# Attention over three layers: scores from 32-row matmuls in four row groups, split probabilities turned by DMA

## The reference

```python
x = x + L0(x)   # softmax(q k^T / sqrt(32)) modulated per head by sigmoid(tanh(..) ..), plus a field term; out @ Wout.T
x = x + L1(x)   # scores = where(mask, -inf, q k^T * scale); softmax; @ v; @ Wo.T; RMS norm of the output, gain and shift
x = x + L2(x)   # norm of x first, softmax attention, @ Wo.T; then a gated MLP behind a second norm
x = x + L3(x)   # quaternion rotation and spectral gate

def _attention(x, Wq, Wk, Wv, Wo):
    q, k, v = (x @ Wq.T), (x @ Wk.T), (x @ Wv.T)      # reshaped to heads
    p = softmax(einsum('blhd,bmhd->bhlm', q, k) / scale)
    return einsum('bhlm,bmhd->blhd', p, v) @ Wo.T
```

## Time and profile before

| | us |
|---|---|
| median of 2 runs | 3087.95 |
| the profiled execution | 3084.3 |
| its span, first to last instruction | 3082.5 |
| PE busy in the span | 2981.2 (97%) |
| DVE busy | 2096.0 (68%) |
| ACT busy | 1394.7 (45%) |
| POOL busy | 621.2 (20%) |
| mean granted PE clock | 0.982 of full speed |

### The profile page before, as it was taken

One profiled execution on the slowest core, in us unless ns is written; L12 is line 12 of the kernel. 1 busy time (PEld: TensorE's weight loads), 2 busy tenths in 40 slices (PEclk: granted clock), 3 DMA queues, 4 the chain that ended last, 5 costly groups with the idle time before them and its releaser, 6 DMA issues. The chain is left out here.

```text
span 3082.5 us, 67681 instructions
## 1 busy us (share of the span) xinstructions
PE 2981.2 (97%) x25333; PEld 2690.0 (87%) x25333; DVE 2096.0 (68%) x3768; ACT 1394.7 (45%) x2236; POOL 621.2 (20%) x434
## 2 busy tenths in 40 slices
PE   6999999999999999989999999599999999999997
PEld 5999999999999999978999999488888888888886
DVE  5777677767788888888888887554454454665554
ACT  3444444445566666666666665332222242222221
POOL 1122212222211111132211112022222221111111
PEclk7999999999999999999999999699999999999999
DMA  5443444345454454544555554322111241111101
GB/s 169 115 110 101 111 107 107 101 116 149 119 134 126 126 135 125 140 131 132 133 138 132 137 131 122 111 99 69 55 55 54 69 138 53 42 41 55 54 28 41
DMA packets 198920, 317.05 MB, mean 103 GB/s; under 512 B 42112, under 2 KB 99584, under 8 KB 198304
## 3 DMA queue, kind: packets, MB, share of 16 engines
q1 hardware_dynamic: 196512, 307.25, 36.2%
q10 hardware_dynamic: 2304, 8.39, 0.9%
HBM read 122.53 MB, written 41.94 MB: 53 GB/s over the span
## 5 line engine op out<-in xcount | busy, mean ns | idle before, releaser
L1642 DVE TENSOR_TENSOR mlp_act_t<-mlp_bank_u,mlp_sg 128x512 f32<-128x512 f32 x128 | 88.5, 691 | 454.3 <-ACT mlp_sg L1544 450.6
L1544 ACT ACTIVATE mlp_sg<-mlp_bank_g 128x512 f32<-128x512 f32 x128 | 76.6, 598 | 632.6 <-PE mlp_bank_u L1457 632.4
L1034 DVE TENSOR_REDUCE att_top<-att_bank_s 128x4 f32<-128x512 f32 x384 | 263.9, 687 | 143.4 <-PE att_bank_s L697 139.5
L1684 POOL TENSOR_TENSOR mlp_al<-mlp_act_t,mlp_ah 128x512 fp32r<-128x512 f32 x128 | 174.8, 1366 | 856.3 <-ACT mlp_ah L1550 856.3
L870 ACT ACTIVATE att_pth<-att_bank_t 128x512 f16<-128x512 f32 x384 | 227.8, 593 | 242.2 <-PE att_bank_t L706 241.9
L875 ACT ACTIVATE att_shifted<-att_shifted,keep_lift 128x512 f32<-128x512 f32 x384 | 276.1, 719 | 105.3 <-DVE att_shifted L1038 103.4
L1042 DVE TENSOR_TENSOR att_ptl<-att_bank_t,att_pth 128x512 f16<-128x512 f32 x384 | 262.0, 682 | 45.4 <-ACT att_pth L870 45.2
L1038 DVE TENSOR_TENSOR att_shifted<-att_bank_s,att_top 128x512 f32<-128x512 f32 x384 | 265.5, 692 | 16.6
L706 PE MATMUL att_bank_t<-keep_pack,att_shifted 128*128 128x128 f32 x1536 | 246.2, 283 | 18.0 <-ACT att_shifted L875 17.8
L1235 POOL TENSOR_TENSOR att_vr<-att_vf,keep_v 128x512 f32<-128x512 f32 x96 | 109.0, 1135 | 731.4 <-ACT keep_v L902 731.4
L651 PE MATMUL att_bank_a<-att_xh,att_wkh 128*128 128x256 f32 x768 | 229.2, 298 | 14.0 <-DVE att_xl L1131 14.0
(11 more groups left out here) (270 smaller groups left out, 8765.5 us busy)
## 6 DMA issues: line engine op xcount, KB each, us to landing
att_ks<-att_kh SPq DMA_DIRECT2D x768, 64.0 KB, 2.0
att_qs<-att_qh SPq DMA_DIRECT2D x768, 64.0 KB, 2.0
att_ks<-att_kl SPq DMA_DIRECT2D x384, 64.0 KB, 2.0
att_qs<-att_ql SPq DMA_DIRECT2D x384, 64.0 KB, 2.0
resid<-att_xres SPq DMA_DIRECT2D x47, 512.0 KB, 2.9
att_xf<-resid SPq DMA_DIRECT2D x32, 512.0 KB, 3.7
mlp_xf<-resid SPq DMA_DIRECT2D x32, 512.0 KB, 4.6
mlp_res<-resid SPq DMA_DIRECT2D x32, 512.0 KB, 4.6
```

The costliest lines, as they stand in the source:

```text
L1034: nc.vector.reduce_max(top[:, u % 2, :], src, AX_X).then_inc(top_ready, 1)
```

## The change

- **Scores.** `qs`, `ks` and `stack` go. `scores` reads `qh`, `ql`, `kh`, `kl` directly: for each head h the 32 rows 32h to 32h + 31, in three steps (high x high, high x low, low x high), each step over the four heads. That is 12 matmuls a unit. `bank_s` is now one tensor over four banks, one head in each; it is single, so a unit's scores wait for the shift of the unit just before.
- **Probabilities.** ACT and DVE split them before they are turned, out of `shifted` in SBUF into `pq` (two buffers). One DMA from SP turns both parts of a unit (256 KB) into `pt` (four buffers, `TURNED`). `weigh_values` of unit u runs in slot u + 4, not u + 3.
- **Order of fills.** The second halves of k and q of a group run in slots 0 to 2 of its own body, the o fills in 3 and 4, then the next group's. `turn_output(i, 1)` moves to slot 1 of the next body, `norm_sum` to slots 7 (`post`) and 9 (`pre`).
- **Other engines.** In layer 2 the load of x for i + 2 is issued on SP after the sixth transpose, ACT squares it in slot 7, DVE adds in slot 8; `norm_end` moves to slots 0 and 1 of the next body, ahead of `shift_scores`. The three splits of v run in slots 0 and 1 of their own body. New weights are loaded by SP into five spare tiles. The mask becomes bf16 and is put in by four matmuls of 128 columns.

The diff, cut to its core:

```diff
-        bank_s = [bank("bank_s0"), bank("bank_s1")]
-        bank_t = [bank("bank_t0"), bank("bank_t1")]
+        bank_s = ctx.enter_context(nc.psum_tensor("att_bank_s", [P, 4, 512], F32))[:, :, 0:P]
...
-        pth, ptl = sb("pth", [P, 2, 4, P], F16), sb("ptl", [P, 2, 4, P], F16)
+        pq = sb("pq", [P, 2, 2, 4, P], F16)
+        pt = sb("pt", [P, TURNED, 2, 4, P], F16)
...
         def fills_of(i):
-            return [("o", 0), ("o", 1), ("k", 0), ("q", 0), ("k", 1), ("q", 1)] + ([("c", 0), ("c", 1)] if lay(i + 1) == 0 else []) + [("v", 0), ("v", 1)]
+            keys, values = [("k", 0), ("q", 0)], [("v", 0), ("v", 1)]
+            ahead = values + keys if values_first(i) else keys + values
+            return [("k", 1), ("q", 1), ("o", 0), ("o", 1)] + ([("c", 0), ("c", 1)] if lay(i + 1) == 0 else []) + ahead
...
-            spans = [2, 2, 2, 2, 2, 1, 1, 1, 2, 2, 2, 1] if len(fills) == 10 else [2, 2, 2, 1, 1, 1, 1, 1, 2, 1, 1, 1]
+            spans = [2, 1, 1, 2, 2] + ([2, 2, 2, 2, 2, 1, 1] if len(fills) == 10 else [1, 1, 1, 1, 2, 1, 1])
...
+            def turn_probs(i, u):
+                n = UNITS * i + u
+                if positive(n - TURNED + 1):
+                    sp.wait_ge(pv_done, n - TURNED + 1)
+                    sp.sem_inc(turn_begun, 1)
+                sp.wait_ge(p_low, n + 1)
+                sp.sem_inc(turn_begun, 1)
+                sp.dma_start_transpose(pt[:, u % TURNED].rearrange("p n h j -> p (n h) j"),
+                                       pq[:, u % 2].rearrange("p n h j -> p (n h j)")).then_inc(turned[u % TURNED], 16)
...
             def body(i):
-                if has(i, 2):
-                    load(i + 2)
+                for u in range(UNITS):
+                    turn_probs(i, u)
+                    if u == 1 and post(i):
                         load_residual(i - 1)
+                    if u == 4 and positive(i) and not post(i):
                         store(i - 1)
+                    if u == 5 and has(i, 2):
+                        load(i + 2)
+                    for n in swaps(i, u, LOAD_AT):
+                        ws.load(sp, n)
...
-                if positive(n - 1):
-                    pe.wait_ge(shift_done, n - 1)
+                if positive(n):
+                    pe.wait_ge(shift_done, n)
                 if u % 4 == 0:
-                    pe.wait_ge(stacked[m], STACKED * (i + 1))
+                    pe.wait_ge(a_free[0], a_done(i, ("k", m)))
+                    pe.wait_ge(a_free[1], a_done(i, ("q", m)))
                 if masked:
-                    nc.tensor.matmul(bank_s[u % 2][:].rearrange("p (h j) -> p h j", h=4), k["ident_r"][:], bcast_mid(k["mask"][:], 4),
-                                     start=True, stop=False)
-                for h in range(4):
-                    q_h, k_h = (t[:, m, h, c % 2, b * P:(b + 1) * P] for t in (qs, ks))
-                    mm = nc.tensor.matmul(bank_s[u % 2][:, h * P:(h + 1) * P], q_h, k_h, start=not masked, stop=not masked or h == 3)
+                    for h in range(4):
+                        nc.tensor.matmul(bank_s[:, h, :], k["ident_b"][:], k["mask"][:], start=True, stop=False)
+                at = slice(b * P, (b + 1) * P)
+                for step, (q_t, k_t) in enumerate(((qh, kh), (qh, kl), (ql, kh))):
+                    for h in range(4):
+                        rows = slice(HD * h, HD * (h + 1))
+                        mm = nc.tensor.matmul(bank_s[:, h, :], q_t[rows, c, at], k_t[rows, c, at], start=step == 0 and not masked, stop=step == 2)
...
                 for s in range(SLOTS):
+                    if s == 1 and not (isinstance(i, int) and i == 0):
+                        turn_output(i - 1, 1)
+                    if s == 3 and lay(i) == 0:
+                        coherence(i)
+                    if s == 6 and lay(i) == 0:
                         sum_values(i, 0)
+                    if s == 7 and post(i):
                         norm_sum(i, 0, i - 1)
+                    if s == 9 and pre(i):
                         norm_sum(i, 1, i + 2)
+                    if s == 10:
                         turn_output(i, 0)
...
                     if s < UNITS:
                         scores(i, s)
+                    if s >= 4:
+                        weigh_values(i, s - 4)
+                    if not at_last:
                         project_pieces(pieces[s])
...
             def high_probs(i, u):
                 n = UNITS * i + u
-                act.wait_ge(t_full, n + 1)
-                if positive(n - 1):
-                    act.wait_ge(pv_done, n - 1)
-                nc.scalar.activation(pth[:, u % 2], bank_t[u % 2][:].rearrange("p (h j) -> p h j", h=4), ACT.Copy).then_inc(p_high, 1)
+                act.wait_ge(exp_done, n + 1)
+                if u >= 2:
+                    act.wait_ge(turned[(u - 2) % TURNED], 16 * (UNITS // TURNED * i + (u - 2) // TURNED + 1))
+                elif positive(UNITS * i):
+                    act.wait_ge(turned[(u - 2) % TURNED], 16 * (UNITS // TURNED * i))
+                nc.scalar.activation(pq[:, u % 2, 0], shifted[:, u % 2], ACT.Copy).then_inc(p_high, 1)
...
+                    if s == 7 and pre(i):
                         act.wait_ge(x_loaded, 16 * (i + 3))
                         squares(norm_turn(1, i + 2), xf[:])
-                    if s == (9 if post(i) else 6) and pre(i):
+                    if s == 9 and pre(i):
                         deviation(i, 1, i + 2)
...
+                    if s < 2 and positive(i) and has(i, 1) and pre(i - 1):
+                        norm_end(i + 1, s)
+                    if s == 2 and positive(i):
+                        low_output(i - 1, 1)
                     if s < UNITS:
                         shift_scores(i, s)
...
+                    if s in (5, 7, 9, 11):
+                        normalise(i, (s - 5) // 2)
...
-                    if s == 4 and post(i):
+                    if s == 6 and post(i):
                         norm_gains(0, i - 1)
                         add_squares(norm_turn(0, i - 1))
...
-                    if s == (7 if post(i) else 4) and pre(i):
+                    if s == 8 and pre(i):
                         norm_gains(1, i + 2)
                         add_squares(norm_turn(1, i + 2))
```

299 lines of the change are left out of this document (108 added, 191 removed).

## The result

The changed kernel takes **3313.18 us**, median of 2 runs (3312.35 to 3314.00), against 3087.95: a ratio of 1.0729 with a 95% interval of 1.0683 to 1.0776. It is slower, as forecast, inside the range, and 58 us above the forecast of 3255 us. Its profiled execution has a span of 3312.2 us, 229.7 more than the 3082.5 of before.

What follows compares the result with a forecast made beforehand. PE bounds the kernel by sheer work, with DVE close behind in layer 2. Less PE work plus new waits gave +11, +18 and +138 us for layers 0, 1 and 2: 3088 + 167 = 3255 us, range 2960 to 3510.

Steps and rivals of the forecast that it cites:

- that number decides this case: In a layer 2 body DVE has only 5.5 us to spare beside PE; this was claimed to settle the outcome.
- TensorE stays the bound: Rival, chance 0.15: one slot of lead suffices everywhere, so only PE's saved work counts, 124 us less, 2964 us.
- a unit of 0.65 us: Score unit on PE if tiling-mode changes drain TensorE twice, 0.16 us each; sum said to be 33 us higher.
- the likeliest case: The forecast case, chance 0.40: PE waits lengthen bodies, mostly in layer 2; 3255 us, own range 3170 to 3340.
- (a): PE's scores wait for DVE's shift 1.8, 1.2, 3.3 us, value matmuls for normalise 1.4, 1.8, 0.4 (layers 0, 1, 2).
- (b): Layer 2, norm_sum: x is loaded late, after the sixth transpose on SP, so PE waits 4.8 to 5.7 us.
- (c): Layer 2, turn_output in slot 10: ACT reads the v fill before the square root, so PE waits 2.7 us.
- (d): Layer 1's norm_sum in slot 7 waits 1.8 us; layer 0 waits 0.8 us for reads of fills and add_field.
- (e): ACT's copy waits for the transpose two units back; up to 3.5 us this only adds 0.7 us at slot 4.
- rival of slow transposes: Chance 0.20: a transpose takes 6 us, so the copy, subtraction and transpose loop decides; +420 us, 3508 us.
- row groups one after another: Rival, chance 0.08: PE's score matmuls do not overlap, 1.2 us a unit; +331 us, 3419 us.
- the threshold of 4.2 us: Transpose time above which the ACT, DVE and DMA loop decides, every further us adding 0.5 us per unit.

Runs made afterwards that it cites:

- four_pq: Changed kernel with four buffers instead of two for the split probabilities ahead of the transposing DMA: 3305.41 us, ratio 1.0704.
- two_turns: Changed kernel with every transposing DMA issued twice, the extra one first into a spare tile, ACT waiting for both: 3434.49 us, ratio 1.1122.

## Why the prediction was right, and where its sum was off

**What bounds the kernel, and the side.** Right in that PE had no slack before and that layer 2 was where it broke. Not borne out: "that number decides this case", of DVE's 5.5 us to spare. DVE's busy time in a body of layer 2 hardly moved (29.81, 29.96 and, cured, 29.88 us), and with it the body takes 47.8 or 36.6 us by order alone; DVE itself sat idle 4.48 us while the long wait built up.

**PE's work: mis-sized.** I had 41.5, 34.4 and 32.6 us a body (and carried 40.2, 34.2 and 32.3 in the sum, by my tables of slots, without showing the step). At full clock it is 42.7, 36.5 and 34.4, higher by 1.2, 2.1 and 1.8. The unit of scores took 0.58 us and not 0.45 (8 x 0.13 = 1.0), and the four mask matmuls 0.33 us for 0.24 (8 x 0.09 = 0.7, layer 1 only); 0.2 to 0.8 us a body is left without a name. Against the busy times of the earlier trace rows, PE saves 1.4, 0.6 and 0.9 us a body, not 2.7. So with every wait gone the change would be worth 16 x 1.4 + 14 x 0.6 + 16 x 0.9 = 45 us, and the rival "TensorE stays the bound" (2964 us) could not have come. The 33 us that I gave for a unit of 0.65 us don't come out of the steps shown either: 0.20 x 8 x 46 would be 74 us of PE's work. Nor does the lower end of the likeliest case's range: 3255 - 50 is 3205, not 3170.

**(a) Waits for the shift and for `normalise`: too high.** I had 3.2, 3.0 and 3.7 us for the layers 0, 1 and 2; measured were about 0.1, 1.7 and 0.9. The slots are uneven, but my tables of slots made more of it than there was, and in layer 2 the 0.9 us stayed when the larger waits were cured. These errors and those in PE's work largely cancel, and that is luck.

**(b) and (c), the two causes in layer 2: right in place, (b) not in its sum.** The waits were 6.1 us where I had 4.8 to 5.7, and 2.5 where I had 2.7, at the places and behind the instructions named, and cured by moving those instructions. But the terms shown for (b), 10.8 us less PE's 6.9, give 3.9 us, and the 5.7 in the sum was not worked out. Measured from slot 6's first score (1747.04) to `norm_sum` (1760.72) the chain is 13.7 us, and PE's part 7.6. The load went out 5.2 us after the start of slot 6, not 4.1, and between the squares and DVE's sums stand the copy of the q fill and two subtractions, 1.7 us, which I had left out. So the near hit of 5.7 on 6.1 is in part luck, and an earlier load alone gave 2.0 of the 6.1 us.

**(d)** 1.2 us in layer 1 for 1.8, none in layer 0 for 0.8. **(e)** A transpose lands in 2.8 us for my 3.5, and the loop costs next to nothing at that (four_pq); with 4.1 us for two, bodies grew, so the threshold of 4.2 us was perhaps too high (two_turns). The rival of slow transposes is out with the 2.8 us, and that of row groups one after another with the 0.58 us. (The upper bound for a transpose was misread: the slowest 512 KB loads on the page of before take 8.3 us, not 6.8. Nothing hung on it.)

**DVE's subtraction** (L1021) was priced 0.69 us and takes longer in the mean, against L1042, the same subtraction before (busy us, mean ns):

```profile
L1021 DVE TENSOR_TENSOR att_pq<-att_shifted,att_pq 128x512 f16<-128x512 f32 x384 | 323.9, 843 | 7.1 <-ACT att_pq L863 7.1
L1042 DVE TENSOR_TENSOR att_ptl<-att_bank_t,att_pth 128x512 f16<-128x512 f32 x384 | 262.0, 682 | 45.4 <-ACT att_pth L870 45.2
```

It takes 0.68 to 0.69 us in all 274 cases with no POOL work beside it. Of the 110 with POOL work beside it 82 are longer, from 0.82 to 2.9 us. Before, with one operand in PSUM, 49 had POOL work beside them and none was longer. So with both operands in SBUF this operation costs DVE 62 us more in all; what of that reached the path was not measured.

**The clock: left out of the sum.** I wrote that a wait near 5 us can also drop the clock and gave it 20 us, beside the sum. The earlier trace rows had shown it once. It costs 3.9 us in each of the 11 steady bodies of layer 2, 43 us, which is the largest part of the 58 us between forecast and result. A forecast of a 5.7 us wait should have carried it in the sum: 16 bodies x 2.5 us would have been 40.

**Group by group:** forecast +11, +18, +138; measured +7.9, +35.1, +183.9 (bodies 1 to 15, 16 to 29, 30 to 45). In layer 1 the body grew by 2.3 us for my 1.3 (39.46, and 40.32 in three of thirteen bodies, where the clock drops). The third group is 46 us above its forecast, about what the clock cost in its steady bodies. The five on the way into layer 2 I had taken as ordinary ones: the first with layer 2's norm (30) grew by 8.4 us (45.96 for 37.55), and the next four by 38.5 together, near my 5 x 8.6 = 43, but by other waits. In those four PE waits 51.5 us, where before it waited 18.6: 30.0 at `norm_sum`, 8.1 at output transposes, 6.4 for shifts, and 6.0 in one score on the low part of q. The cure for steady bodies hardly shortened 31 and 32, and what would was not tested.

## What to carry to other kernels

When a change takes a little work off the engine that bounds the kernel and reorders all others to do so, count first what the move of each instruction puts behind it in its queue: here that was 200 us, and the work saved at most 45. Such a wait on TensorE costs itself and the stretch at 1.2 GHz behind it (here waits of 6.1 and 2.5 us in a body brought 3.9 us more), and that belongs in the sum. Where the bounding engine waits for a result, put a piece of its independent work ahead of the wait: moving `norm_sum` so gave 1.2 us a body in layer 1 (38.5 to 37.3) and 0.7 in layer 2 (36.6 to 35.9).
